# Degrees' copy, third merge, last gelu and first chunk in the order around a graph kernel's first relational layer

## The reference, cut to what matters

```python
def _L0_gnn_ref(x, edge_index, W, b, gamma, beta):
    h = _gcn_conv(x, edge_index, W, b)      # degrees -> deg**-0.5, x @ W.T, sums over edges
    h = _batch_norm(h, gamma, beta)         # over the 625 nodes
    h = jax.nn.gelu(h, approximate=False)
    return h + identity

def rgcn_gate_layer(x, row, col, edge_type, basis, att, gate_w, root, bias):
    w = jnp.einsum('rb,bio->rio', att, basis)          # 30 bases of 512x512 -> 2 relations
    x_j = x[col]
    for r in range(NUM_RELATIONS):
        gate = jax.nn.sigmoid(x_j @ gate_w[r, :, 0])
        msgs.append(gate[:, None] * x_j @ w[r])
    msg = jnp.where((edge_type == 0)[:, None], msgs[0], msgs[1])
    agg = jax.ops.segment_sum(msg, row, num_segments=x.shape[0])
    return agg + x @ root + bias

x = _layernorm(x + _L0_gnn_ref(...), axis=-1)
h = relu(rgcn_gate_layer(x, ..., basis1, ...)); out = rgcn_gate_layer(h, ..., basis2, ...)
x = _layernorm(x + out, axis=-1)
```

## Time and profile before

| | us |
|---|---|
| median of 3 runs | 292.68 (292.48 to 292.92) |
| the profiled execution's own time | 294.33 |
| its span | 292.5 |
| TensorE busy in the span | 267.5 (91%) |
| VectorE busy | 167.3 (57%) |
| ScalarE busy | 82.9 (28%) |
| GpSimd busy | 50.0 (17%) |

### The profile page before, as it was taken

One profiled execution on the slowest core, in us unless ns is written; L12 is line 12 of the kernel. 1 busy time (PEld: TensorE's weight loads), 2 busy tenths in 40 slices (PEclk: granted clock), 3 DMA queues, 4 the chain that ended last, 5 costly groups with the idle time before them and its releaser, 6 DMA issues.

```text
span 292.5 us, 4587 instructions
## 1 busy us (share of the span) xinstructions
PE 267.5 (91%) x1661; PEld 179.3 (61%) x1661; DVE 167.3 (57%) x361; ACT 82.9 (28%) x141; POOL 50.0 (17%) x92
## 2 busy tenths in 40 slices
PE   0899997999889987999999999999999999999990
PEld 0793433434576753646455477777787778787870
DVE  6788878887748789966847333121432243234443
ACT  2451021001436976354166310220032331000000
POOL 5521000000394102012332000000009000011111
PEclk9999999999979999999999999999999999999999
DMA  6999999999799969879999998883004200001112
GB/s 161 221 403 412 384 409 406 407 403 335 290 362 313 384 223 411 369 294 420 422 420 390 420 393 323 322 325 156 3 0 121 61 0 0 0 2 35 35 35 70
DMA packets 12964, 74.15 MB, mean 253 GB/s; under 512 B 2035, under 2 KB 2278, under 8 KB 4749
## 3 DMA queue, kind: packets, MB, share of 16 engines
q1 hardware_dynamic: 11330, 70.82, 63.2%
q0 software_dynamic: 1264, 2.87, 3.6%
q10 hardware_dynamic: 346, 0.17, 0.2%
HBM read 72.57 MB, written 1.28 MB: 252 GB/s over the span
## 4 chain that ended last, share of the span: by engine, by line
PE 66%; DVE 15%; issue 6%; DMA 6%; DVEq 2%; POOL 2%; ACT 1%; POOLq 0%; ACTq 0%
PE psW L561 14%; PE psM L542 10%; PE psM L544 9%; PE psM L543 9%; PE psM L819 8%; PE psM L845 6%; DMA basis_ring<-in_L_gnn_basis_dram 6%; PE psM L691 3%; DVE B L1174 3%; PE psE L648 2%; PE psM L615 2%; DVEq L1164 2%; DVE w_full L1151 1%; DVE oh_key L1181 1%; DVE oh_src L1181 1%
## 5 line engine op out<-in xcount | busy, mean ns | idle before, releaser
L561 PE MATMUL psW<-basis_ring,S 128*32 128x512 f32 x512 | 62.3, 599 | 1.1 <-DMA basis_ring<-in_L_gnn_basis_dram 0.7
L1351 DVE SCALAR_TENSOR_TENSOR zg<-psM,gate,zg 125x512 fp32r<-125x512 f32 x20 | 15.0, 751 | 33.6 <-ACT zg L1007 33.0
L561 PEld LDWEIGHTS psW<-basis_ring,S 128*32 128x32 f32 x512 | 12.8, 108 | 28.2 <-issue 19.4
L648 PEld LDWEIGHTS psE<-oh_key,oh_src 128*125 128x125 f16 x162 | 13.9, 143 | 19.9 <-issue 16.0
L819 PE MATMUL psM<-BB,zg 125*128 125x320 f32 (+1 forms) x160 | 24.3, 306 | 0.0
L845 PE MATMUL psM<-zg,BB 125*125 125x512 f32 x100 | 24.0, 394 | 0.0
L819 PEld LDWEIGHTS psM<-BB,zg 125*128 125x128 f32 x160 | 23.4, 189 | 0.0
L1174 DVE TENSOR_TENSOR B<-B,psE 125x160 f32 x54 | 17.4, 323 | 8.4 <-issue 2.8
L845 PEld LDWEIGHTS psM<-zg,BB 125*125 125x125 f32 x100 | 18.5, 185 | 4.7
L648 PE MATMUL psE<-oh_key,oh_src 128*125 128x160 f16 x162 | 17.2, 245 | 3.8 <-DVE B L1174 3.6
L615 PE MATMUL psM<-w0T,xT 128*125 128x512 f32 x40 | 20.3, 609 | 0.0
(11 more groups left out here) (165 smaller groups left out, 443.6 us busy)
## 6 DMA issues: line engine op xcount, KB each, us to landing
basis_ring<-in_L_gnn_basis_dram SPq DMA_DIRECT2D x64, 1024.0 KB, 7.5
root_raw<-in_L_gnn_root_dram POOLq DMA_DIRECT2D x32, 64.0 KB, 3.0
xs<-in_x_dram SPq DMA_DIRECT2D x1, 1120.0 KB
out_dram<-xs SPq DMA_DIRECT2D x5, 224.0 KB
w_raw<-in_L_gnn_W_dram SPq DMA_DIRECT2D x4, 256.0 KB, 9.3
gate_raw<-in_L_gnn_gate_w_dram POOLq DMA_DIRECT2D x2, 250.0 KB, 6.5
bias_b<-in_L_gnn_bias_dram POOLq DMA_DIRECT2D x1, 250.0 KB, 3.7
xs<-in_x_dram SPq DMA_DIRECT2D x1, 130.0 KB
```

The lines of the kernel that those rows point to most:

```text
L561: m = nc.tensor.matmul(psW[32 * j:32 * j + 32, cc % 2, :], S[:, cc % 2, cc // CH, q].rearrange("p k r -> p (k r)"), ring[:, n % RING, j, : ...
L648: nc.tensor.matmul(psE[0:PC, g % 2, at:at + KEYS], oh_src[:, g % 3, j * P:j * P + PC], oh_key[:, t % OH, :], start=(j % SG == 0), stop=(j ...
L1351: link(v.scalar_tensor_tensor(out=zg[:, 1, c, r, :], in0=bank(("Z", L, c, r))[0:PC, :], scalar=gate[:, L, c, r:r + 1], in1=zg[:, 0, c, r, ...
```

## The change

It has five parts. The degrees' copy goes in front of the second merge's shuffle. `w_merge(2)` goes from behind block 2's statistics to behind block 1's, and `w_low(1)` takes its place. The last gelu is two instructions, of the columns of chunks 0 and 1 and of the rest. Chunk 0 is normalised by VectorE with mean and root (no offset from GpSimd), half of `w_low(2)` goes behind that, and `residual_sum(2)` goes behind `w_merge(3)`, `residual_sum(3)` behind `w_low(3)`. The turned chunk 0 is put in two banks of psE and split into its parts in two halves, and TensorE starts on blocks 0 and 1 of relation 0 after the first half.

```diff
--- before.py
+++ after.py
@@ -230,6 +230,7 @@
         t_hi, t_ready = sem("t_hi"), sem("t_ready")
         root_hi, root_ready = sem("root_hi"), sem("root_ready")
         x1_turned = sem("x1_turned")
+        first_hi, first_lo = sem("first_hi"), sem("first_lo")
         gw_ready = sem("gw_ready")
         gate1_in, gate_q_ready, gate_dots = sem("gate1_in"), sem("gate_q_ready"), sem("gate_dots")
         gate_rows_ready, gate_ready = sem("gate_rows_ready"), sem("gate_ready")
@@ -355,6 +356,8 @@
                 eng.wait_ge(at_ready, [a for a in range(NC) if a not in SUMMED].index(c) + 1)
 
         FIRST_IN = 23
+        GELU_FIRST = 2 * PC
+        HALF_K = KC // 2
 
         def turned_from(i):
 
@@ -512,6 +515,9 @@
 
             for c in range(NC):
                 pool.wait_ge(var_ready, KC + 1 + c)
+                if c == 0:
+                    inverse_root(lrs[:, 0:1], 1)
+                    continue
                 link(nc.gpsimd.tensor_tensor(lrs[:, c:c + 1], lrs[:, c:c + 1], mhalf[0:PC, 0:1], ALU.pow))
                 nc.gpsimd.tensor_tensor(lnm[:, 1, c:c + 1], lnm[:, 0, c:c + 1], lrs[:, c:c + 1], ALU.mult) \
                     .then_inc(rstd_ready, 1)
@@ -725,7 +731,7 @@
                 basis_upto((None, FIRST_IN + 2, FIRST_IN + 3, FIRST_IN + 5)[f])
             def way_back(f, c):
 
-                pe.wait_ge(gelu_done, f + 1)
+                pe.wait_ge(gelu_done, f + 1 + (f == KC - 1 and (c + 1) * PC > GELU_FIRST))
                 if f == 0:
                     wait_free(pe, ("g", c))
                 last[0] = nc.tensor.transpose(bank(("g", c))[0:PC, f * P:(f + 1) * P],
@@ -746,7 +752,8 @@
                 if c >= 2:
                     pe.wait_ge(t_ready, c - 1)
                 for k in range(KC):
-                    last[0] = nc.tensor.transpose(psE[:, c % 2, k * PC:(k + 1) * PC], xs[:, c, k * P:(k + 1) * P],
+                    b, at = (c % 2, k) if c else (k // HALF_K, k % HALF_K)
+                    last[0] = nc.tensor.transpose(psE[:, b, at * PC:(at + 1) * PC], xs[:, c, k * P:(k + 1) * P],
                                                   ident[0:PC, 0:PC])
                 last[0].then_inc(x1_turned, 1)
 
@@ -789,9 +796,11 @@
 
             x1_turns(0)
             basis_upto(32)
+            pe.wait_ge(first_lo, 1)
+            z_product(0, 0, 0, range(0, HALF_K))
             pe.wait_ge(t_ready, 1)
-            for r in range(R):
-                z_product(0, 0, r, range(0, KC - 1))
+            z_product(0, 0, 0, range(HALF_K, KC - 1))
+            z_product(0, 0, 1, range(0, KC - 1))
             x1_turns(1)
             for r in range(R):
                 z_product(0, 0, r, range(KC - 1, KC))
@@ -955,8 +964,9 @@
                     w_high(2)
                 if f:
                     act.wait_ge(bn_ready, f)
-                    nc.scalar.activation(hf[:, f - 1, :], hf[:, f - 1, :], ACT.Gelu, bias=bn[:, 1, f - 1:f],
-                                         scale=bn[:, 0, f - 1:f]).then_inc(gelu_done, 1)
+                    for n in ((slice(0, GELU_FIRST), slice(GELU_FIRST, N)) if f == KC else (slice(0, N),)):
+                        nc.scalar.activation(hf[:, f - 1, n], hf[:, f - 1, n], ACT.Gelu, bias=bn[:, 1, f - 1:f],
+                                             scale=bn[:, 0, f - 1:f]).then_inc(gelu_done, 1)
             w_first(3)
             def root1_high(k):
 
@@ -979,8 +989,11 @@
 
             act.wait_ge(free_act, releaser[:uses[("bb", NBB - 1)] + 1].count("act"))
             nc.scalar.activation(gate[:, 1, 0], mhalf[0:PC, 0:R], ACT.Sigmoid)
-            x1_out(0)
-            x1_hi(0)
+            act.wait_ge(x1_turned, 1)
+            for k, ready in ((slice(0, HALF_K), first_hi), (slice(HALF_K, KC), t_hi)):
+                nc.scalar.activation(hlT[:, 0, k, 0:PC],
+                                     psE[:, k.start // HALF_K, 0:HALF_K * PC].rearrange("p (k n) -> p k n", k=HALF_K),
+                                     ACT.Copy).then_inc(ready, 1)
             x1_out(1)
             w_high(3)
 
@@ -1143,8 +1156,16 @@
 
             def w_merge_rest(pp):
 
+                w_merge_second(pp)
+                w_merge_swap(pp)
+
+            def w_merge_second(pp):
+
                 link(v.scalar_tensor_tensor(out=half[:, 1, :], in0=psW[:, 1, :], scalar=mask_h[:, 0:1],
                                             in1=half[:, 1, :], op0=ALU.mult, op1=ALU.add))
+
+            def w_merge_swap(pp):
+
                 to, swapped = w_full(pp, 1), half[:, 1, :]
                 if pp < KC:
                     to, swapped = in_q(to), natural(swapped)
@@ -1152,9 +1173,9 @@
                 dve.sem_inc(w_both, 1)
                 dve.sem_inc(w_merged, 1)
 
-            def w_low(pp):
-
-                for r in range(R):
+            def w_low(pp, types=range(R)):
+
+                for r in types:
                     dve.wait_ge(w_hi, R * pp + r + 1)
                     upper, lower = (w_block(pp // KC, pp % KC)[:, r, i, :] for i in range(2))
                     v.tensor_tensor(lower, w_full(pp, r), upper.bitcast(F32), ALU.subtract).then_inc(w_lo, 1)
@@ -1256,11 +1277,13 @@
 
             for c in (1, 2, 0, 3, 4):
                 counts_of(c)
-            w_merge(1)
+            w_merge_first(1)
+            w_merge_second(1)
             wait_full(dve, "deg")
             link(v.tensor_copy(deg[:], bank("deg")[0:PC, 0:2 * NC:2]))
             dve.sem_inc(free_dve, 1)
             dve.sem_inc(deg_ready, 1)
+            w_merge_swap(1)
             for c in range(NC):
                 dve.wait_ge(dinv_ready, 1 if c == 0 else 2)
                 dve.wait_ge(z_hi, c + 1)
@@ -1295,10 +1318,12 @@
                     dve.wait_ge(vec_ready, 1)
                 link(v.tensor_tensor(bn[:, 3, e], bag[:, f, 0:1], vecT[:, f, V_B:V_B + 1], ALU.add))
                 link(v.tensor_tensor(bn[:, 3, e], vecT[:, f, V_B:V_B + 1], bn[:, 3, e], ALU.subtract))
-                if f < 2:
-                    w_low(f)
-                if f == 2:
+                if f == 0:
+                    w_low(0)
+                elif f == 1:
                     w_merge(2)
+                elif f == 2:
+                    w_low(1)
             bn_finish(KC - 1)
 
             def statistics(c, full):
@@ -1354,17 +1379,42 @@
                 dve.sem_inc(free_dve, 1)
                 dve.sem_inc(zg_ready, 1)
 
-            w_low(2)
+            def statistics_begun(c):
+
+                v.bn_stats(lst[:, c, :], x_sum[:, c, :]).then_inc(vchain, 1)
+                chained[0] += 1
+                return chained[0]
+
+            def spread_ended(c, known):
+
+                dve.wait_ge(vchain, known)
+                link(v.bn_aggr(lag[:, c, :], lst[:, c, :]))
+                if c:
+                    v.tensor_scalar(lnm[:, 0, c:c + 1], lag[:, c, 0:1], -1.0, None, ALU.mult)
+                variance(c)
+
+            w_low(2, (0,))
             residual_sum(0)
-            spread_of(0, lambda: residual_sum(1))
-            spread_of(1, lambda: residual_sum(2))
+            known0 = statistics_begun(0)
+            residual_sum(1)
+            spread_ended(0, known0)
+            known1 = statistics_begun(1)
+            dve.wait_ge(rstd_ready, KC + 1)
+            v.tensor_scalar(xs[:, 0, :], x_sum[:, 0, :], lag[:, 0, 0:1], lrs[:, 0:1], ALU.subtract, ALU.mult) \
+                .then_inc(x1_ready, 1)
+            w_low(2, (1,))
+            spread_ended(1, known1)
             dve.wait_ge(free_act, releaser[:uses[("bb", NBB - 1)] + 1].count("act"))
             v.memset(hlT[:, :, :, N:N2].bitcast(F32), 0.0)
-            w_merge_first(3)
-            x1_lo(0)
-            w_merge_rest(3)
+            for k, upper, lower in ((slice(0, HALF_K), (first_hi, 1), first_lo), (slice(HALF_K, KC), (t_hi, 1), t_ready)):
+                dve.wait_ge(*upper)
+                v.tensor_tensor(hlT[:, 1, k, 0:PC],
+                                psE[:, k.start // HALF_K, 0:HALF_K * PC].rearrange("p (k n) -> p k n", k=HALF_K),
+                                hlT[:, 0, k, 0:PC].bitcast(F32), ALU.subtract).then_inc(lower, 1)
+            w_merge(3)
+            residual_sum(2)
+            w_low(3)
             residual_sum(3)
-            w_low(3)
             residual_sum(4)
             x1_lo(1)
             spread_of(2)
```

## The result

The changed kernel took 298.02 us (median of 6 runs, 295.98 to 299.63) and the kernel before 293.12 beside it (6 runs, 292.48 to 294.41): ratio 1.0154, 95% interval 1.0108 to 1.0199. I had forecast 291.8, faster, so both the sign and the size are wrong. Twice more on other chips it was 297.52 against 293.37 (1.0109, 1.0066 to 1.0153) and 297.95 against 293.16 (1.0121, 1.0063 to 1.0180). The profiled execution took 295.98, with a span of 294.1. It is the fastest of its six, so its trace shows less than the median lost.

What follows compares the result with a forecast made beforehand. TensorE, busy 91% of the span, was taken to bound the kernel. Products start 3.3 us sooner, a new bank wait gives back 2.3, so gain 0.94: 292.68 to 291.74, said as 291.8; range 290.2 to 292.8.

Steps and rivals of the forecast that it cites:

- the part on the degrees' copy: Copy ahead of the second merge's shuffle: 0.67 us gained, the delay of two basis parts (77.59 to 78.59) hidden in gaps.
- basis loads that are issued as the parts there are used, so they move with it: Behind basis part start 123.89: same work in both kernels, with loads moving along, so an earlier start moves the end.
- Third merge: w_merge(2) one block sooner: last sum 1.37 us sooner, and the 0.59 us bank wait at 105.38 goes.
- Gelu in two: Last gelu, start 2.85 us behind the last sum: first piece about 0.60 us instead of 0.92, residual_sum(0) at 108.2 against 110.49.
- Chunk 0 on VectorE: Normalising chunk 0: power ends 3.92 us behind residual_sum(0), normalising takes 0.54, PE turns at 112.8, 2.8 us sooner.
- Halves: Split of turned chunk 0: PE busy in part 32 until +1.6 us, products start at 114.4, 3.3 us sooner.
- The bank of g2: Z(0,0,1) needs the bank residual_sum(2) frees, now behind w_merge(3): new 2.3 us PE wait (the bank wait), until 118.85.
- Behind it: From Z(0,0,1) at 118.85, 15 products and the turning take 4.11 us; basis parts start at 122.95 against 123.89.
- 1: Rival: the bank wait does not bite and PE waits for w_low(3); gain 2.7 us, to 290.0; chance 0.07.
- 2: Rival: the shuffle and GpSimd's power block each other, or smaller slips add up; 292.8, no change; chance 0.17.
- 3: Rival: granted clock falls behind the 2.3 us wait at 116.55, Z's products cost 1.6 us more; 293.3, slower; chance 0.10.
- 4: Rival: the clock's fall at 83.65 goes, as PE waits 0.6 less ahead; 1.5 us more gained, 290.3; chance 0.08.

Runs made afterwards that it cites:

- half_loads: The changed kernel with basis loads 22 to 35 bringing only the first half of each row: 294.42 us, 1.0026 of the kernel before.
- after_again: The changed kernel as it is, timed again on another chip: 297.52 us against 293.37 for the kernel before, ratio 1.0109.
- bank_free: The changed kernel with psW's bank handed back once the merge has read it, not after its shuffle: 292.89 us, 0.9957 of the kernel before.
- root_late: The changed kernel with GpSimd's 16 root1 loads moved behind chunk 1's power: 297.54 us, 1.0134 of the kernel before.

## Why the prediction was wrong

- **The step that failed:** "The delay thus falls into gaps that exist", in the part on the degrees' copy. I had the copy right (76.82, I said 76.95), and parts 20 and 21 nearly (78.85, I said 78.59), but took them at 1.86 us. They took 3.64, as the granted clock had fallen to half, and load 24, which waits for part 20, came late with them. The last sum came at 105.36 instead of 104.23, 1.1 us late. I had told of such a fall at 83.65 in the trace of before, and priced a new one only behind the bank wait.
- **The second that failed:** "basis loads that are issued as the parts there are used, so they move with it" was looked at behind 123.89 alone. Between 100 and 118 us I moved parts 28 to 32 by 1 to 3 us ahead with no bound for their loads. After, parts 30, 31 and 32 begin 2.48 and 2.58 us apart (111.70, 114.18, 116.76): that is the pace of 1 MB at 416 GB/s, not that of TensorE. half_loads shows it: no waits for loads there, and the loss is a quarter or less (1.0026 against 1.0109 to 1.0154). Chunk 0 was ready at 114.07 and turned at 115.72, so this step adds 1.65 us. The two make up nearly all of the 2.77 us by which part 33 was later than my sum (125.72 against 122.95).
- **What that leaves open.** Against the kernel before the profiled execution lost 1.65 us, and the medians 4.2 to 4.9. after_again's trace, at 297.69 near its median, has part 33 at 126.79, 2.9 us later than before, with 4.8 us of waits for loads instead of 3.0. How the rest is made up isn't known.
- **Third merge:** right. The first sum was at 99.33, 3.10 behind the merge's start; from the first block's first sum (88.81) to the last it was 16.55 us against 106.27 - 88.28 = 17.99: 1.44 sooner, I said 1.37. No bank wait at the count transposes of the last block.
- **Gelu in two:** the start right (105.36 + 2.85 = 108.21); the pieces took 1.19 together; the sum came 1.35 behind the gelu's start where I had 1.12, as TensorE's turning was later by part 28's load.
- **Chunk 0 on VectorE:** right: 113.52 - 109.56 = 3.96 (I had 4.0), 0.55 long.
- **Halves:** the first product came 2.03 behind the turning and not 1.6, as part 32, ahead of it, waited 0.45 for its load.
- **The bank of g2:** right, and the one place where the order of banks had to be read. From the turning to Z(0,0,1) it took 5.90 after, 5.96 in half_loads and 6.03 in bank_free; I had 6.05. The wait was 1.49 and not 2.3 only because the products came late.
- **Behind it:** 4.10 (I had 4.11), and the same 168.4 to the end.
- **Rivals.** 1 fell: the wait is there. 2 fell: GpSimd's two powers took 1.56 us beside the shuffle as before without it. By the Trainium skill, SBUF — State Buffer, "SBUF: two separate sides", one SBUF input does not take the shared pair, and the trace agrees. 3 was seen in root_late's trace, not in the three traces of the kernel after. Whether the slowest of its executions have it isn't known. 4 was the wrong way round: the fall didn't go but came sooner and lasted 6.8 us. It did go in bank_free, where waits for loads used up what it gave.

## What to carry to other kernels

A ring of loads turns a delay of one consumer into a delay of every load behind it, and where the DMA engines are at their full rate it is not made up. So before a step is put ahead of the signal that frees a buffer, ask what that signal releases, and give the buffer back where its last reader ends rather than where the block of work ends. When a sum moves a stretch ahead, move its loads with it and check them, with every other load that runs beside them, against the DMA rate there, in the stretch and not only behind it. And when a variant lands on the forecast's number, compare the steps too: here two of them were off by 1.3 and 1.5 us and cancelled.

## What the runs showed of the hardware

The granted clock fell at different times in executions of the same kernel: 76.6, 77.8 and 78.05 us in the kernel after's three, for 6.8 us each, and 82.8 for 3.4 in that of before. The Trainium skill, TensorE: Matmul & The Clock Gate, "Part 1: The HAM clock gate", says that the gate's watching doesn't start with the kernel and that cold stretches differ from run to run. These traces agree with the second; no run here shows the first. For a forecast it means that a stretch in which TensorE does little has a chance of half clock behind it, and that the price is what stands just behind: 1.7 us on two basis parts, 1.6 us on the products behind the bank wait.
